# One block for three phases: the cross-attention's first loads, maxima and products moved in among the last steps of the self-attention

## The chip, the cores and the metric

The kernel runs on one core of a Trainium2 chip. The metric is the device time of one execution in microseconds, smaller being better. The core has TensorE (PE, matrix products, with its weight loads as PEld), VectorE (DVE), ScalarE (ACT), GpSimd (POOL) and SyncE (SP), which here only issues DMAs. Each engine works through its own list of instructions in order, and they meet at semaphores.

## The reference, cut to what matters

A decoder layer with normalisation after each part, over 32 sequences of 128 rows and 512 features:

```python
x = layernorm(x + attn(x, Wq, Wk, Wv, Wo))      # 16 heads of 32, rope, causal
x = layernorm(x + xattn(q=x, k=ctx, v=ctx))     # 8 heads; a head is 16 rows of the
                                                # sequence, and the 512 features take the
                                                # place of the positions
x = layernorm(x + ffn(x))                       # two ternary-weight layers, 512-2048-512
```

In `xattn` the scores of a head are a 512 by 512 matrix (contracted over 16 rows), so a sequence needs 8 such matrices, their row maxima, exponentials, and products with the values.

## The kernel before

The kernel has three phases: the self-attention, the cross-attention and the feed-forward. All loops are over the 32 sequences (`NB`) and are written out; inside a phase, `step(t)` of each engine works on several sequences at once, each at another stage.

The self-attention is a block of its own. Its results go to memory: `x1` (scratch x1), and `x1` and the context split in two parts of fewer bits (scratch x_part, c_part), in which the cross-attention later reads a head's rows as a stack. A block ends with all engines meeting: SP waits for the last stores (`x1_st`, `part_st`, `cpart_st`), and only then does the second block begin, which holds the cross-attention and the feed-forward. The order of work in the last steps of the self-attention is, on DVE: `out_low(31)` (L451), `norm_x1(30)` (L491), `residual(31)` (L475), `statistics(31)` (L479 to L484), `norm_x1(31)`. On PE: `attend(31)` (L599), `out_projection(31)` (L537). On POOL: `split_x1(30)` (L258, L293), `power(31)` (L300), `split_x1(31)`. On SP: x loads (L210), c_part stores (L214), x1 stores (L219) and x_part stores (L204). `norm_x1(b)` waits for the store of x1(b-1) to land, and `split_x1(b)` for the store of x_part(b-1), since each has one buffer.

The cross-attention's opening, in the second block, is:

- POOL fills the rows of ones: eight fills of 32 x 1024 in `cs` (L830) and two of 128 x 512 in `vT` (L834).
- SP loads four stacks, for sequences 0 and 1 in two groups of heads each: `load_stacks` issues eight DMAs for each (L739, L743), 768 KB by their shapes. Between them it loads ident, gamma and `cT`.
- For sequence 0, 16 units: PE forms two 512-wide products into a half of `wide` (`max_unit`, L987), and DVE takes their maxima (`pair_max`, L930). There are two halves, so PE is two units ahead at most.
- After unit 9, which needs the first nine maxima, PE transposes the first group's maxima (`transpose_max`, L994), ACT evicts them (L897), and POOL splits them (L857, L860) and writes them with four DMAs into the stacks (`store_max`, L867). Unit 10 waits for ACT's eviction.

Then the steady part begins: in a step of sequence b, eight `n` of four score tiles each (PE L1034, ACT's exponentials L906), products with the values (L1017), and the next sequence's 16 units of maxima between them. Its first scores wait for the first `store_max`, and those of n = 4 for the second one, `store_max(0, 0, 1)`, which POOL makes of maxima transposed after n = 0.

During steps 3 to 10 of the self-attention ACT also sums the magnitudes of the feed-forward's weights, into a tile `magnitude` of 2048 columns (L414).

Of the kernel before, what the change touches and what calls it, by code (L numbers as in the profile page):

```python
# [74 lines left out]
def self_attention(nc, NB, t_in, scratch, w_stage, w_abs):  # L75
# [5 lines left out]
    with ExitStack() as ctx:  # L81
        def sb(name, shape, dt=F32):
            return ctx.enter_context(nc.sbuf_tensor("a_" + name, shape, dt))

        def sem(name):
            return ctx.enter_context(nc.semaphore("a_" + name))

        stage = [w_stage[:, n * F:(n + 1) * F].rearrange("p (c n) -> p c n", c=KC) for n in range(4)]
        magnitude = sb("magnitude", [P, F])
        w_hi = sb("w_hi", [P, KC, 3 * D], F32R)  # L90
        w_lo = sb("w_lo", [P, KC, 3 * D], F32R)
        wo_hi = sb("wo_hi", [P, KC, D], F32R)
        wo_lo = sb("wo_lo", [P, KC, D], F32R)
        ident = sb("ident", [P, P])
        ident_b = sb("ident_b", [P, P], BF16)
        mask4 = sb("mask4", [P, HPC, P], BF16)
        cos = sb("cos", [P, DH])
        sin = sb("sin", [P, DH])
        xT = sb("xT", [P, D])
        xT_hi = sb("xT_hi", [P, KC, P], F32R)  # L100
        xT_lo = sb("xT_lo", [P, KC, P], F32R)
        x = sb("x", [P, D])
        q_raw = sb("q_raw", [P, D])
        q_sin = sb("q_sin", [P, D])
        q_rot = sb("q_rot", [P, D])
        k_sin = sb("k_sin", [P, D])
        k_cos = sb("k_cos", [P, D])
        k_rot = sb("k_rot", [P, D])
        v = sb("v", [P, KC, HPC, DH])
        qT = sb("qT", [P, KC, P])  # L110
        kT = sb("kT", [P, KC, P])
        neg_max = sb("neg_max", [P, HPC, KC])
        prob = sb("prob", [P, HPC, KC, P])
        probT = sb("probT", [P, HPC, KC, P])
        den = sb("den", [P, HPC, KC])
        rden = sb("rden", [P, HPC, KC])
        oT_hi = sb("oT_hi", [P, KC, P], F32R)
        oT_lo = sb("oT_lo", [P, KC, P], F32R)
        x1_sum = sb("x1_sum", [P, D])
        bn = sb("bn", [P, 6])  # L120
        mv = sb("mv", [P, 2])
        vare = sb("vare", [P, 1])
        neg_half = sb("neg_half", [P, 1])
        rstd = sb("rstd", [P, 1])
        x1 = sb("x1", [P, D])
        x1_part = sb("x1_part", [P, PARTS, D], F32R)
        c_in = sb("c_in", [P, D])
        c_part = sb("c_part", [P, PARTS, D], F32R)

        bank = [ctx.enter_context(nc.psum_tensor(f"a_bank{i}", [P, D], F32)) for i in range(8)]  # L130
        s_ps, (v_ps, q_ps, k_ps, o_ps) = bank[:4], bank[4:]

        w_ld = [sem(f"w_ld{n}") for n in range(4)]
        const_ld = sem("const_ld")
        w_hi_done = sem("w_hi_done")
        w_lo_done = sem("w_lo_done")
        pool_const = sem("pool_const")
        xT_ld = sem("xT_ld")
        x_ld = sem("x_ld")
        c_ld = sem("c_ld")  # L140
        x1_st = sem("x1_st")
        part_st = sem("part_st")
        cpart_st = sem("cpart_st")
        xT_hi_done = sem("xT_hi_done")
        xT_split = sem("xT_split")
        q_proj = sem("q_proj")
        k_proj = sem("k_proj")
        v_proj = sem("v_proj")
        q_raw_done = sem("q_raw_done")
        v_done = sem("v_done")  # L150
# [102 lines left out]
        def _(pool):  # L253
# [60 lines left out]
            def step(t, on):  # L314
# [4 lines left out]
                if on(0):  # L319
                    split_xT(t)  # L320
# [1642 lines left out]
```

## Time and profile before

| what | value |
|---|---|
| median of 3 runs | 1864.62 us (1862.95 to 1865.49) |
| the profiled execution's own time | 1859.43 us |
| its span, first to last instruction | 1857.6 us |
| PE busy | 1606.8 us (86%) |
| DVE busy | 1545.5 us (83%) |
| ACT busy | 1373.7 us (74%) |
| POOL busy | 959.0 us (52%) |
| mean granted TensorE clock | 0.931 |

The profile is of one execution, 0.3% shorter than the median run. Times in the trace count from the first instruction. A granted clock of 1.00 is 2.4 GHz, and 0.50 is 1.2 GHz; a value between is a stretch with both.

### The profile page before, as it was taken

The numbers are of one execution on the slowest core, as the hardware profiler recorded it, in microseconds if no ns is written. First come the engines' busy times: TensorE is split into PE (matmuls) and PEld (weight loads), VectorE is DVE, ScalarE is ACT, GpSimd is POOL, SyncE is SP. The second block draws the span as 40 slices with busy tenths as digits, with TensorE's granted clock in tenths as the row PEclk, the third lists the DMA queues.
The fourth block names the chain that finished last, engine by engine and source line by source line (L and its number), as shares of the span: only waits on it lengthen the run. The fifth ranks groups of instructions, "written<-read, shape, count | busy, mean of one in ns | idle before, by whom it ended". The sixth has DMA issues, their size and how long they took to land.

```text
span 1857.6 us, 35125 instructions
## 1 busy us (share of the span) xinstructions
PE 1606.8 (86%) x11936; PEld 873.5 (47%) x12000; DVE 1545.5 (83%) x2086; ACT 1373.7 (74%) x2837; POOL 959.0 (52%) x1407
## 2 busy tenths in 40 slices
PE   6999999999995498999999999999857777767784
PEld 4777777777774133333333333333323333333331
DVE  4778888888885597999999999999579999989985
ACT  4666654555553187888888888888789999989994
POOL 4666767767664443255553555423445555545552
PEclk9999999999998598999999999999988888888887
DMA  3455443443443445444456544444333333333311
GB/s 139 140 187 173 119 135 107 124 131 107 128 124 111 97 107 107 107 122 113 109 145 183 151 121 121 108 116 124 93 106 104 105 103 103 108 97 103 112 53 34
DMA packets 119268, 217.09 MB, mean 117 GB/s; under 512 B 32241, under 2 KB 34705, under 8 KB 116785
## 3 DMA queue, kind: packets, MB, share of 16 engines
q1 hardware_dynamic: 110770, 213.64, 40.8%
q0 software_dynamic: 8320, 1.21, 0.4%
q8 instruction: 96, 1.57, 0.4%
q14 instruction: 82, 0.67, 0.1%
HBM read 137.67 MB, written 76.02 MB: 115 GB/s over the span
## 4 chain that ended last, share of the span: by engine, by line
PE 32%; issue 11%; ACT 7%; DVE 6%; DMA 5%; POOL 4%; SPq 1%; POOLq 0%; DVEq 0%; ACTq 0%
PE sums L1017 13%; PE bank L1034 11%; PE wide L987 6%; DMA out<-c_result 3%; DVE stage L1658 2%; ACT stage L1543 2%; ACT b_prob L906 2%; DMA b_xs<-b_max_part 2%; DVE b_smax L930 1%; POOL c_up_rstd L1391 1%; DVE c_x L1645 1%; POOL c_mid_rstd L1426 1%; PE wide L994 1%; POOL b_xs L867 1%; DVE c_x_rnd L1699 1%
## 5 line engine op out<-in xcount | busy, mean ns | idle before, releaser
L930 DVE TENSOR_REDUCE b_smax<-wide 128x2 f32<-128x1024 f32 x512 | 620.3, 1225 | 67.5 <-PE wide L987 55.5
L906 ACT ACTIVATE b_prob<-bank 128x512 f32<-128x512 f32 x1024 | 556.3, 599 | 108.2 <-PE bank L1034 98.3
L1034 PE MATMUL bank<-b_xs,b_cs 50*128 50x512 f32 x1024 | 328.0, 475 | 22.5 <-ACT b_prob L906 12.8
L1017 PE MATMUL sums<-b_prob,b_vT 128*32 128x256 f32 (+1 forms) x3584 | 316.0, 424 | 5.5 <-ACT b_prob L906 0.5
L987 PE MATMUL wide<-b_cs,b_xs 48*128 48x512 f32 x1024 | 283.6, 439 | 37.7 <-DMA b_gamma<-in_gamma 30.9
L1836 PE MATMUL sums<-c_w,c_hqT 128*128 128x512 bf16 x481 | 168.9, 527 | 113.5 <-issue 104.0
L1034 PEld LDWEIGHTS bank<-b_xs,b_cs 50*128 50x128 f32 x1024 | 132.8, 186 | 230.2 <-ACT b_prob L906 168.6
L857 POOL TENSOR_SCALAR b_max_part<-b_neg_max 16x128 fp32r<-16x128 f32 x64 | 18.6, 290 | 337.0 <-ACT b_neg_max L897 337.0
L371 ACT ACTIVATE a_prob<-a_bank,a_neg_max 128x128 f32<-128x128 f32 x512 | 181.9, 418 | 3.6 <-DVE a_neg_max L459 3.6
L1836 PEld LDWEIGHTS sums<-c_w,c_hqT 128*128 128x128 bf16 x512 | 63.2, 128 | 209.1 <-issue 183.4
L987 PEld LDWEIGHTS wide<-b_cs,b_xs 48*128 48x128 f32 x1024 | 128.5, 191 | 64.8 <-POOL b_vT L834 31.3
L867 POOL DMA_DIRECT2D b_xs<-b_max_part x256 | 134.1, 530 | 42.1 <-POOL b_max_part L860 37.2
L1017 PEld LDWEIGHTS sums<-b_prob,b_vT 128*32 128x32 f32 x3584 | 72.6, 108 | 164.2 <-issue 106.6
L467 DVE TENSOR_TENSOR a_prob<-a_prob,a_rden 128x512 f32<-128x512 f32 x128 | 144.8, 1131 | 4.4
L349 ACT ACTIVATE a_v<-a_bank 128x512 f32<-128x512 f32 x32 | 19.1, 598 | 171.7 <-PE a_bank L599 171.7
L371 ACT ACTIVATION_READ_ACCUMULATOR a_prob<-a_bank,a_neg_max 128x1 f32 x512 | 132.3, 258 | 0.0
L1824 PE MATMUL wide<-c_w,c_xqT 128*128 128x512 bf16 x510 | 121.0, 392 | 0.5 <-issue 0.5
L537 PE MATMUL a_bank<-a_w_hi,a_xT_hi 128*128 128x512 f32 x384 | 108.2, 404 | 11.9 <-POOL a_xT_lo L269 11.9
L537 PE MATMUL a_bank<-a_w_lo,a_xT_hi 128*128 128x512 f32 x384 | 103.8, 392 | 0.0
L537 PE MATMUL a_bank<-a_w_hi,a_xT_lo 128*128 128x512 f32 x384 | 103.8, 392 | 0.0
L258 POOL TENSOR_SCALAR a_x_part<-a_x 128x512 fp32r<-128x512 f32 x32 | 19.9, 622 | 157.8 <-DMA scratch_x_part<-a_x_part 155.4
L587 PE MATMUL a_bank<-a_ident,a_prob 128*128 128x128 f32 x512 | 79.7, 282 | 10.1 <-DVE a_prob L467 9.4
(147 smaller groups left out, 3240.7 us busy)
## 6 DMA issues: line engine op xcount, KB each, us to landing
scratch_c_part<-a_c_part SPq DMA_DIRECT2D x64, 256.0 KB
scratch_x_part<-a_x_part SPq DMA_DIRECT2D x64, 256.0 KB
b_xs<-scratch_x_part SPq DMA_DIRECT2D x128, 128.0 KB, 3.1
b_cs<-scratch_c_part SPq DMA_DIRECT2D x128, 128.0 KB, 3.1
scratch_heads<-b_heads SPq DMA_DIRECT2D x64, 256.0 KB, 2.5
a_xT<-in_xT SPq DMA_DIRECT2D x32, 256.0 KB, 6.7
a_c_in<-in_ctx SPq DMA_DIRECT2D x32, 256.0 KB, 2.6
a_x<-in_x SPq DMA_DIRECT2D x32, 256.0 KB, 4.1
```

Source lines behind the costliest of these rows:

```text
L371: last = act.activation(prob[:, j, c, :], s_ps[j][:, c * P:(c + 1) * P], ACT.Exp, bias=neg_max[:, j, c:c + 1], accum_out=den[:, j, c:c + 1])
L467: dve.tensor_tensor(prob[:, j, :, :], prob[:, j, :, :], rden[:, j, :].unsqueeze(2).broadcast_to([P, KC, P]), ALU.mult).then_inc(norm_done, 1)
L537: last = pe.matmul(out, a[:, c, :], b[:, c, :], start=(n == 0), stop=(n == 3 * KC - 1))
L587: last = pe.transpose(s_ps[j][:, c * P:(c + 1) * P], prob[:, j, c, :], ident[:, :])
L867: pool.dma_start(xs[p][g][row:row + 1, :, :].rearrange("r h q -> r (h q)").bitcast(F32), max_part[g][2 * KC * e:2 * KC * (e + 1), j, :].bi ...
L906: act.activation(prob[k % 8][:, :], e_ps[bank_of(k)][:, :], ACT.Exp, scale=0.25).then_inc(exp_done, 1)
L930: dve.tensor_reduce(smax[g][:, :, j, qc], m_ps[u % 2][:, :, :], AX.X, ALU.max, negate=True).then_inc(max_done, 1)
L987: last = pe.matmul(m_ps[u % 2][:, e, :], xs[p][g][half(e, STACK), j, qc * P:(qc + 1) * P], cs[p][g][half(e, STACK), j, :], start=True, sto ...
L1017: last = pe.matmul(av_ps[2 * XD * h:2 * XD * (h + 1), cols], vT[p][:, lc, XG * g + h, :], prob[(XG * n + 2 * j + e) % 8][:, cols], start=( ...
L1034: pe.matmul(e_ps[bank_of(2 * u + e)][:, :], cs[p][g][half(e), j, lc * P:(lc + 1) * P], xs[p][g][half(e), j, :], start=True, stop=True).the ...
L1824: last = pe.matmul(h_ps[:, n, :], xqT[:, c, :], w1[:, c, n * D:(n + 1) * D], start=False, stop=(c == KC - 1))
L1836: last = pe.matmul(y_ps[:, :], hqT[:, c, :], w2[:, c, :], start=(c == 0), stop=(c == FC - 1))
```

## The change

The cross-attention's opening is handed to the self-attention as a function `begin` for each engine. The one block that is left has no meeting of the engines inside it. What moves, engine by engine:

- POOL: all ten fills stand ahead of everything else. `values(0, 0)` comes after step 33, `store_max(0, 0, 0)` after `power(31)`, and `split_x1(31)` behind that. Then POOL waits for all stores of the self-attention, writes four small constants and goes on with `store_max(0, 0, 1)`.
- SP: ahead of step 32 the stacks of sequence 0, ident, gamma and `cT`; ahead of step 33 one stack of sequence 1, and ahead of step 34 the other.
- PE: units 0 and 1 ahead of `out_projection(31)`, the 14 others behind it.
- DVE: maxima 0 to 3, `norm_x1(30)`, maxima 4 and 5, `residual(31)` and `statistics(31)`, maxima 6 to 9, `norm_x1(31)`, maxima 10 to 15.

What goes with it: `load_stacks` waits for the stores of its sequence, the feed-forward's loads wait for x1's, the score tiles of both attentions lie in the same PSUM tensor `wide`, the self-attention's tiles share their SBUF with tiles used later (`late`), and `magnitude` becomes a stack's tile of half the width, so that each sum of magnitudes is made in two halves.

```diff
     def sync(sp, begin):
...
             for t in range(NB, NB + 5):
+                begin(t - NB)
                 step(t, lambda k: t - k < NB)
-            sp.wait_ge(x1_st, 16 * NB)
-            sp.wait_ge(part_st, 16 * PARTS * NB)
-            sp.wait_ge(cpart_st, 16 * PARTS * NB)
...
     def gpsimd(pool, begin):
-            pipeline(pool, NB, 4, step)
+        for t in range(NB + 2):
+            step(t, lambda k: 0 <= t - k < NB)
+        begin(0)
+        step(NB + 2, lambda k: k > 2)
+        begin(1)
+        step(NB + 3, lambda k: k > 3)
...
     def scalar(act):
-                    act.activation(magnitude[:, :], w_stage[:, c * F:(c + 1) * F], ACT.Abs,
-                                   accum_out=w_abs[:, m, c:c + 1]).then_inc(ffn_summed, 1)
+                for half in range(2):
+                    at = c * F + half * F // 2
+                    if 2 * i + half > 0:
+                        act.wait_ge(ffn_summed, 2 * i + half)
+                    act.activation(magnitude, w_stage[:, at:at + F // 2], ACT.Abs,
+                                   accum_out=w_abs[:, m, 2 * c + half:2 * c + half + 1]).then_inc(ffn_summed, 1)
...
     def vector(dve, begin):
-            pipeline(dve, NB, 3, step)
+        for t in range(NB + 1):
+            step(t, lambda k: 0 <= t - k < NB)
+        out_low(NB - 1)
+        begin(0, 4)
+        norm_x1(NB - 2)
+        begin(4, 6)
+        residual(NB - 1)
+        statistics(NB - 1)
+        begin(6, 10)
+        norm_x1(NB - 1)
+        begin(10, XH * KC // 2)
...
     def tensor(pe, begin):
-            pipeline(pe, NB, 2, step)
+        for t in range(NB + 1):
+            step(t, lambda k: 0 <= t - k < NB)
+        begin(0, 2)
+        out_projection(NB - 1)
+        begin(2, XH * KC // 2)
...
def cross_attention(nc, ctx, NB, t_in, scratch, psum, sems, weights):
...
         def load_stacks(s, p, g):
+            sp.wait_ge(sems["part_st"], 16 * PARTS * (b + 1))
+            sp.wait_ge(sems["cpart_st"], 16 * PARTS * (b + 1))
+        def begin(k):
+            if k == 0:
                 sp.wait_ge(ones_done, 2)
                 load_stacks(0, 0, 0)
...
-        for g in range(2):
-            sp.wait_ge(ones_done, 6 + 2 * g)
-            load_stacks(0, 1, g)
+            if k in (1, 2):
+                sp.wait_ge(ones_done, 4 + 2 * k)
+                load_stacks(0, 1, k - 1)
...
     def gpsimd(pool):
+        def begin(k):
+            if k == 0:
                 values(0, 0, first=True)
+            if k == 1:
                 store_max(0, 0, 0, first=True)
+        def main():
+            for n in ("part_st", "cpart_st"):
+                pool.wait_ge(sems[n], 16 * PARTS * NB)
+            pool.wait_ge(sems["x1_st"], 16 * NB)
+            weights["of"].constants(pool)
...
     def tensor(pe):
+        def main():
+            pe.wait_ge(sems["sum_done"], NB)
             pairs(pe, pair)
```

## Rows read from the trace of the kernel before

**Rows 1.** The windows view: busy time, granted clock (PEclk), DMA share, GB/s

```profile
613.00:640.65 27.65, 12.15 (x33) 4.92 (x35) 16.75 (x16) 0.27 (x1) 12.53 (x21) 0.50 0.72 137
```

**Rows 2.** The waits, 560 to 640 us: total, times, longest

```profile
PE wide L987 <- DMA b_gamma<-in_gamma: 30.9, 1, 30.9
POOL a_x_part L258 <- DMA scratch_x_part<-a_x_part: 21.8, 3, 9.4
```

**Rows 3.** The timeline, all engines, 585 to 640 us: start, duration, engine, line

```profile
587.73 0.69 DVE L451 TENSOR_TENSOR a_oT_lo<-a_bank,a_oT_hi 128x512 fp32r<-128x512 f32 x1 [0.67 <-ACT a_oT_hi L386]
587.95 3.08 SPq L204 DMA_DIRECT2D scratch_x_part<-a_x_part  x2
...
590.49 1.08 PE L537 MATMUL a_bank<-a_wo_hi,a_oT_lo 128*128 128x512 f32 x4
594.09 0.55 DVE L491 TENSOR_SCALAR a_x<-a_x_sum,a_mv,a_rstd 128x512 f32<-128x512 f32 x1 [5.66 <-DMA scratch_x<-a_x]
...
594.77 0.69 DVE L475 TENSOR_TENSOR a_x_sum<-a_bank,a_x 128x512 f32<-128x512 f32 x1
...
596.55 0.15 DVE L484 TENSOR_SCALAR a_vare<-a_mv 128x1 f32<-128x1 f32 x1
597.08 0.62 POOL L258 TENSOR_SCALAR a_x_part<-a_x 128x512 fp32r<-128x512 f32 x1 [9.38 <-DMA scratch_x_part<-a_x_part]
...
599.00 0.56 POOL L300 TENSOR_TENSOR a_rstd<-a_vare,a_neg_half 128x1 f32<-128x1 f32 x1
...
605.34 0.62 POOL L258 TENSOR_SCALAR a_x_part<-a_x 128x512 fp32r<-128x512 f32 x1 [5.78 <-DMA scratch_x_part<-a_x_part]
...
613.03 7.96 POOL L830 MEMSET b_cs<- 32x1024 f32 x8 [5.72 <-POOLq L81]
...
615.00 0.80 SPq L739 DMA_DIRECT2D b_xs<-scratch_x_part  x2
...
621.05 1.12 POOL L834 MEMSET b_vT<- 128x512 f32 x2
...
622.50 1.22 PE L987 MATMUL wide<-b_cs,b_xs 48*128 48x512 f32 x4 [30.92 <-DMA b_gamma<-in_gamma]
...
623.40 11.41 DVE L930 TENSOR_REDUCE b_smax<-wide 128x2 f32<-128x1024 f32 x10 [10.21 <-PE wide L987]
...
634.60 0.29 POOL L857 TENSOR_SCALAR b_max_part<-b_neg_max 16x128 fp32r<-16x128 f32 x1 [6.29 <-ACT b_neg_max L897]
...
635.39 9.15 DVE L930 TENSOR_REDUCE b_smax<-wide 128x2 f32<-128x1024 f32 x8 [0.58 <-PE wide L987]
636.08 2.35 POOL L867 DMA_DIRECT2D b_xs<-b_max_part  x4 [0.66 <-POOL b_max_part L860]
```

**Rows 4.** SP's waits, 500 to 640 us

```profile
SPq L198 <- POOL a_c_part L293: 39.8, 4, 11.4
```

**Rows 5.** The windows view: n = 0 to 3 of sequence 0, then 4 to 7

```profile
640.65:653.19 12.54, 12.54 (x75) 4.65 (x71) 10.38 (x10) 8.56 (x17) 5.36 (x8) 0.68 0.01 1
653.19:663.90 10.71, 10.39 (x93) 3.94 (x89) 10.00 (x9) 9.56 (x19) 6.71 (x7) 1.00 0.35 101
```

**Rows 6.** The timeline again: the second group's maxima, scores of n = 4

```profile
644.53 0.29 POOL L857 TENSOR_SCALAR b_max_part<-b_neg_max 16x128 fp32r<-16x128 f32 x1 [6.10 <-ACT b_neg_max L897]
...
653.23 0.50 PE L1034 MATMUL bank<-b_xs,b_cs 50*128 50x512 f32 x2
```

**Rows 7.** The timeline of the kernel's first microseconds

```profile
7.64 2.29 DVE L431 TENSOR_TENSOR a_w_lo<-stage,a_w_hi 128x2048 fp32r<-128x2048 f32 x1 [7.64 <-ACT a_w_hi L335]
...
9.37 1.05 POOL L258 TENSOR_SCALAR a_xT_hi<-a_xT 128x512 fp32r<-128x512 f32 x1 [8.55 <-DMA a_mask<-in_mask]
```

**Rows 8.** The page's groups: busy, mean ns, idle before and its releaser

```profile
L349 ACT ACTIVATE a_v<-a_bank 128x512 f32<-128x512 f32 x32 | 19.1, 598 | 171.7 <-PE a_bank L599 171.7
```

**Rows 9.** All instructions of line 414

```profile
L414 ACT ACTIVATE a_magnitude<-stage x8: 1911/1936/1947, 75.2 to 197.4; 128x2048 f32<-128x2048 f32 x8
```

**Rows 10.** The waits, 690 to 760 us

```profile
PE bank L1034 <- DMA b_xs<-b_max_part: 4.5, 1, 4.5
```

More of the change, by code:

```diff
@@ L701, in cross_attention, with late @@
     MAX_LOADS = 2 * PARTS
+    prob, heads = [], []
+    def late():
+        prob.extend(sb(f"prob{i}", [P, D]) for i in range(8))
+        heads.extend(sb(f"heads{g}", [P, D]) for g in range(2))
     def after(s, p):
@@ L788, in step @@
                 load_stacks(s + 1, p, 0)
-            weights.load(sp, s, p, 0)
+            weights["of"].load(sp, s, p, 0)
             if not first:
@@ L821, in rest, with ones @@
                 store_rden(NB - 1)
-        return rest
-    def gpsimd(pool):
+        return begin, main, rest
+    def ones(pool):
         n = 0
@@ L836, in gpsimd @@
             pool.wait_ge(ones_done, n)
-        weights.constants(pool)
+    def gpsimd(pool):
         def values(s, p, first=False):
@@ L970, in rest @@
                 reciprocals(NB - 1)
-        return rest
+        return begin, main, rest
     def tensor(pe):
@@ L1063, in pair, with begin, main @@
             step(s, 1, False, first, last)
-        pe.wait_ge(ones_done, 10)
-        pe.wait_ge(const_ld, 32)
-        for u in range(PAIRS):
-            max_unit(0, 0, u, first=True, after_mt=1 if u == 10 else None)
-            if u == 9:
-                transpose_max(0, 0, 0, 9)
-        pairs(pe, pair)
-        for part in range(2):
-            products(NB // 2 - 1, 1, STEPS - 1, part)
-    return sync, gpsimd, scalar, vector, tensor
+        def begin(u, to):
+            if u == 0:
+                pe.wait_ge(ones_done, 10)
+                pe.wait_ge(const_ld, 32)
+            while u < to:
+                max_unit(0, 0, u, first=True, after_mt=1 if u == 10 else None)
+                if u == 9:
+                    transpose_max(0, 0, 0, 9)
+                u += 1
+        def main():
+            pe.wait_ge(sems["sum_done"], NB)
+            pairs(pe, pair)
+            for part in range(2):
+                products(NB // 2 - 1, 1, STEPS - 1, part)
+        return begin, main
+    return late, ones, (sync, gpsimd, scalar, vector, tensor), xs[1][1]
 def feed_forward(nc, ctx, NB, t_in, scratch, stage, w_abs, psum, sems, out):
@@ L1295, in prepare @@
             if slot == 4:
-                self.fold(pool, w_abs, KC, 0)
+                self.fold(pool, w_abs, 2 * KC, 0)
                 for m in range(2):
@@ L1885, in _ @@
         def _(sp):
-            ffn[0](sp, attn[0](sp))
+            begin, main, rest = attn[0](sp)
+            own[0](sp, begin)
+            main()
+            ffn[0](sp, rest)
         @block.gpsimd
         def _(pool):
-            attn[1](pool)
+            ones(pool)
+            begin, main = attn[1](pool)
+            own[1](pool, begin)
+            main()
             ffn[1](pool)
@@ L1894, in _ @@
         def _(act):
+            own[2](act)
             attn[2](act)
@@ L1899, in _ @@
         def _(dve):
-            ffn[3](dve, attn[3](dve))
+            begin, main, rest = attn[3](dve)
+            own[3](dve, begin)
+            main()
+            ffn[3](dve, rest)
         @block.tensor
         def _(pe):
-            attn[4](pe)
+            begin, main = attn[4](pe)
+            own[4](pe, begin)
+            main()
             ffn[4](pe)
```

1027 lines of the change are left out of this document (515 added, 512 removed).

## The prediction

> **What bounds the kernel now.** I began with the windows view. In each attention's steady part PE sets the pace: n = 0 to 7 of the first sequence of the cross-attention take 12.54 and 10.71 us with PE busy for 12.54 and 10.39 of them [rows 5]. Between the phases it does not: from the second block's start at 613.0 to the first scores at 640.65 PE is busy for 12.15 of 27.65 us, at the lower clock [rows 1]. The waits name the largest hole: PE stood still for 30.9 us before the first maxima's products [rows 2].
>
> The timeline shows what fills that hole. PE's last self-attention product starts at 590.49 and takes 1.08. Behind it runs a chain that uses almost no engine: x1(29)'s store lands at 594.09, DVE normalises and adds until 596.70, POOL splits x1(30) at 597.08 when x_part(29)'s store has landed, its next split waits until 605.34 for x_part(30), and the block ends when x_part(31) has landed; the fills start at 613.03 [rows 2, 3]. Then come ten fills (9.1 us with those of `vT`), the loads, and at 622.50 the first unit. From 623.40 DVE sets the pace: ten maxima in 11.41 us, 1.14 each [rows 3].
>
> **What the change removes.** I follow DVE, since the opening's 16 maxima must all pass through it, and compare the start of maximum 10, which is at 635.39 now [rows 3]. After the change:
>
> - `out_low(31)` ends at 588.42. Units 0 and 1 are by then on PE, which is free behind `attend`, and their stacks were loaded long before. Maxima 0 and 1: until 590.71.
> - Unit 2 stands behind `out_projection(31)`, which ends at 591.57. From unit to maximum it takes 0.90 (622.50 to 623.40), so maxima 2 and 3 run from 592.47 to 594.76 [rows 3].
> - `norm_x1(30)` can run, x1(29) having landed at 594.09. With 0.6 for it: 595.36. Maxima 4 and 5: 597.65.
> - `residual(31)` and `statistics(31)` took 594.77 to 596.70, or 1.93, so 599.6. Maxima 6 to 9: 604.2. `norm_x1(31)`: 604.8.
> - Maximum 10 waits for PE's transpose and ACT's eviction. That path now takes 1.72 from maximum 8's end (623.40 + 9 x 1.141 = 633.67) to 635.39; here from 603.05 to 604.77. It is covered by maximum 9 and the norm [rows 3].
>
> So maximum 10 starts at 604.8, which is 30.6 us earlier, and PE's first scores follow at 610.05 in place of 640.65. Everything behind them keeps its order and moves along. This is the large term: **-30.6**.
>
> **What it adds.** Three chains must be ready for that, and SP and POOL are now shared.
>
> SP: ahead of step 32 it issues 19 DMAs, at 0.46 each 8.7 us (0.80 for the two of [rows 3], and a gap). It waited there up to 11.4 us for the context's split [rows 4], which I take as the cover; without it step 32's loads would be 8.7 us late. Ahead of steps 33 and 34 stand eight DMAs each, 3.7 us. The first eight lie in the wait for `sum_done` behind step 32. The second eight push x_part(29)'s two stores from 587.95 to 591.6. They landed 9.1 us after 587.95 [rows 3]; I keep that figure, so they land at 600.8. It is a choice between 6.3 (x_part(30) was issued as POOL's split ended at about 599.0 and had landed by 605.34), which gives 597.9, and 9.1 plus the stall of the second store's issue again (3.08 for two issues, in place of 0.9), which gives 602.9.
>
> POOL: `split_x1(30)` then takes 600.8 to 602.7 (597.08 to 599.00 before), `power(31)` until 603.3. `norm_x1(31)` wants it at 604.2 and `store_max(0, 0, 0)` wants POOL at 634.60 - 30.6 = 604.0, so 0.7 us is to spare. If x_part(29) lands at 597.9, more; if at 602.9, the opening loses 1.4. I take **0**.
>
> POOL again: x_part(30) is issued at 602.7 and lands 6.3 later, at 609.0; its split ends at 611.0, and x_part(31) lands 5.7 to 6.3 later (before, at most 613.03 - 607.30). POOL stands in front of `store_max(0, 0, 1)` until 616.7 to 617.3, add 0.2 for the constants. From POOL's copy to the first use it took at most 640.65 - 634.60 = 6.05 [rows 3], so its rows are ready at 622.95 to 623.55. The scores of n = 4 came 12.58 after the first ones [rows 5, 6], so they want them at 622.63. Before, this `store_max` began at 644.53, 8.7 us ahead of its use [rows 6]. The new wait on stores costs 0.3 to 0.9; I take the low side, since 6.05 is an upper bound: **+0.3**. Behind POOL's wait stand `values(0, 1)`, needed only a whole step later (12.54 + 10.71 us [rows 5]), and the weights' preparation.
>
> The kernel's start: ten fills of 9.1 us from 0.72 end at 9.8; the first split of xT starts at 9.37 now, beside DVE's subtraction (7.64 to 9.93), and takes 1.05, where the same copy of x1 takes 0.62 [rows 3, 7]. At 9.9 it no longer runs beside it: +0.2 at the least. If DVE's subtraction slows the fills as it slows that copy (1.05 / 0.62, over its 2.3 us), they end 0.9 later: +1.1. PE's first product hangs on that split, with nothing to hide it. I take the middle, **+0.6**.
>
> The shared port has a rule in the Trainium skill (SBUF — State Buffer, Who interferes with whom): a DVE instruction with two SBUF inputs contends with a GpSimd instruction that reads SBUF, not with one that only writes. The trace's 1.05 for the copy beside the subtraction agrees; the fills only write, so by the rule the term would be +0.2 and the sum -30.1.
>
> Magnitudes in halves: eight passes of 1.94 us [rows 9] become sixteen of at least half that, with one more fixed start and a wait each. If each half cost as much as a whole, ACT would have 1.9 us more in eight steps. It idles 171.7 / 32 = 5.4 us a step before `values`, right behind these passes [rows 8]: **0**. Without that idle time it would be 15 us. The two waits in each `load_stacks` are on counts long reached, and one more fold of `w_abs` falls into POOL's idle time (POOL is at 13 of 27 us even in the opening [rows 1]): 0.
>
> The sum is -30.6 + 0.3 + 0.6 = **-29.7 us**. Against the profiled execution's span of 1857.6 this is 1827.9, and its own time is 1.8 longer. The median of the runs shown lies 5.2 above the profiled time (0.3%), so I set the difference against the median: 1864.62 - 29.7 = **1834.9 us**.
>
> **The rivals.**
>
> *POOL's and DVE's chain becomes late.* A store that lands after 601.5 in place of 600.8 costs a microsecond per microsecond, at `power(31)`, and again at the second `store_max`, two stores further. For it: x_part(29) took 9.1, and 768 KB of loads now run ahead of it. Against: the DMA share had room. With 602.9 for the first and 8 in place of 6.3 for the next two, the sum loses 5 to 6: 1840.5. Chance 0.22.
>
> *The first scores' own DMA lands late.* The small stores of maxima are in flight together with x_part(30). Later in the kernel PE waits 4.5 us for one of them [rows 10]; the same here gives 1839.4. Chance 0.06. The Trainium skill (DMA: Bandwidth & Descriptors, Queues, rings and completion order) says that a completion lands only after every earlier write of that DMA engine, across its queues. The 4.5 us fit, but no row here tells that cause from another.
>
> *The clock stays up.* PE now works through the hole, and the main part may begin at the upper clock. The first four n took 12.54 us at a mean clock of 0.68 (half speed for 8.0 us), the next four 10.71 [rows 5]: a gain of 1.8, or 3 if counted with the product that n = 0 lacks. Against: busy for 12.15 of 27.65 us PE stayed at 0.50 [rows 1], and the new order gives it the same two products per maximum. It gives 1832.5. Chance 0.12.
>
> *The loads crowd out the self-attention's own transfers.* Window 613 to 640.65 moved 137 GB/s at a share of 0.72 [rows 1], so four stacks (3.1 MB) fill the DMA engines for 16 us. Laid wholly onto the last steps this returns 16 us, half of it 8: about 1847 in the middle. Against: they are spread over 35 us. Chance 0.08.
>
> *Nothing overlaps:* DVE stands at `norm_x1(30)` with the maxima behind it, until the stores have gone as late as now. The opening then ends where it did: 1864. Chance 0.02.
>
> *Slower: the clock stays down.* If PE, never rested but never full, stays at half speed after the first scores, each microsecond so spent costs 1.83 / 8.0 = 0.23, or 3 / 8.0 = 0.37. It decides from 80 to 130 us of half speed beyond the 8 of now; 170 us of it give 1874 to 1898. Against: PE at full duty came back to 1.00 within the first four n [rows 5]. Chance 0.03.
>
> **How the numbers follow.** The forecast as worked out has 0.47; the rivals 0.22, 0.06, 0.12, 0.08, 0.02 and 0.03. Low end: the clock's 3 us, the start at +0.2, no wait at the stores, and 2 to 3 us of difference between executions (the three runs span 2.5): 1828. High end: 1840.5 with the start at +1.1 and the executions' spread: 1843. That leaves out crowding, no overlap and the slow case, and a little of each side. A difference under 0.2% can't be told from none. Faster: 0.95; within 0.2%: 0.02; slower: 0.03.
>
> **What would show it.** Right: the maxima L930 start near 588.5 and number 10 near 605; the first scores 30 us earlier; `xT_hi` at about 9.9; `store_max(0, 0, 1)` near 617, just in time. PE has no hole of over 5 us near 600. Wrong: DVE idle before `norm_x1(30)` or `(31)` for a DMA, POOL's second `store_max` after 620 with PE waiting at n = 4, last self-attention steps longer than before, or another granted clock in the later phases, which the sum takes as unchanged and which alone could move the time by several microseconds.

## The result, and the profile after

The changed kernel took 1834.56 us (median of 4 runs, 1833.18 to 1843.81) against 1865.05 for the one before (4 runs, 1862.95 to 1869.94) on the same chip: a ratio of 0.985, 95% interval 0.983 to 0.987. The profiled execution took 1833.27 us with a span of 1831.5. A second comparison with more runs (`r1_change`: 6 against 23) gives 1833.02 against 1862.14, ratio 0.985 (0.982 to 0.989). The forecast was 1834.9, faster.

The timeline of the changed kernel for DVE, 585 to 625 us. It answers to [rows 3]; line 969 is the maximum (930 before), 493 the norm of x1, 477 the residual.

```profile
585.03 0.69 DVE L477 TENSOR_TENSOR a_x_sum<-sums,a_x 128x512 f32<-128x512 f32 x1 [1.87 <-PE sums L549]
...
588.25 2.35 DVE L969 TENSOR_REDUCE b_smax<-wide 128x2 f32<-128x1024 f32 x2
591.94 2.36 DVE L969 TENSOR_REDUCE b_smax<-wide 128x2 f32<-128x1024 f32 x2 [1.35 <-PE wide L1029]
594.24 0.55 DVE L493 TENSOR_SCALAR a_x<-a_x_sum,a_mv,a_rstd 128x512 f32<-128x512 f32 x1
594.71 2.35 DVE L969 TENSOR_REDUCE b_smax<-wide 128x2 f32<-128x1024 f32 x2
...
598.81 4.61 DVE L969 TENSOR_REDUCE b_smax<-wide 128x2 f32<-128x1024 f32 x4
...
604.00 6.88 DVE L969 TENSOR_REDUCE b_smax<-wide 128x2 f32<-128x1024 f32 x6
```

The gap of 5.66 us before `norm_x1(30)` is gone: the maxima fill it, and DVE is busy for 22.30 of the 24.91 us from 585 to the first scores. Maximum 10 starts at 604.00, where [rows 3] have 635.39.

The same timeline for POOL and SP: the split of x1 is line 253, `store_max` 885 to 895, the stores of x_part 201, the stacks' loads 764 and 768.

```profile
588.19 2.65 SPq L764 DMA_DIRECT2D b_xs<-scratch_x_part  x2
590.89 1.60 SPq L768 DMA_DIRECT2D b_cs<-scratch_c_part  x2
...
594.39 1.20 SPq L201 DMA_DIRECT2D scratch_x_part<-a_x_part  x2
...
600.69 0.62 POOL L253 TENSOR_SCALAR a_x_part<-a_x 128x512 fp32r<-128x512 f32 x1 [12.43 <-DMA scratch_x_part<-a_x_part]
...
602.62 0.56 POOL L295 TENSOR_TENSOR a_rstd<-a_vare,a_neg_half 128x1 f32<-128x1 f32 x1
603.22 0.29 POOL L885 TENSOR_SCALAR b_max_part<-b_neg_max 16x128 fp32r<-16x128 f32 x1
...
608.56 0.61 POOL L253 TENSOR_SCALAR a_x_part<-a_x 128x512 fp32r<-128x512 f32 x1 [1.37 <-issue]
...
616.82 0.29 POOL L885 TENSOR_SCALAR b_max_part<-b_neg_max 16x128 fp32r<-16x128 f32 x1
```

The stores' chain has not become shorter; the wait that was at the block's end is now spent inside the cross-attention, and POOL comes to the second `store_max` at 616.82. PE's side, same timeline: the first scores and those of n = 4 (line 1076).

```profile
609.91 0.80 PE L1076 MATMUL bank<-b_xs,b_cs 50*128 50x512 f32 x2 [0.44 <-DMA b_xs<-b_max_part]
...
621.70 0.50 PE L1076 MATMUL bank<-b_xs,b_cs 50*128 50x512 f32 x2
```

Its waits, 560 to 640 us, answer to [rows 2]. PE's wait of 30.9 us is gone; what is left is DVE's pace.

```profile
POOL a_x_part L253 <- DMA scratch_x_part<-a_x_part: 23.5, 3, 12.4
...
PE wide L1029 <- DVE b_smax L969: 7.6, 10, 2.3
...
POOL c_neg_half L1324 <- DMA scratch_x_part<-a_x_part: 6.1, 1, 6.1
```

The windows view (PE, PEld, DVE, ACT, POOL busy, granted clock, DMA share, GB/s): first the clock around 596 and after 616 us, then the first four n and the next four, as in [rows 5].

```profile
594.00:596.00 2.00, 0.52 (x4) 0.21 (x4) 2.00 (x4) 0.00 (x0) 0.00 (x0) 0.99 0.84 178
596.00:598.00 2.00, 1.57 (x4) 0.56 (x4) 1.97 (x3) 0.00 (x0) 0.00 (x0) 0.50 0.68 189
...
616.00:618.00 2.00, 2.00 (x22) 0.51 (x14) 1.08 (x2) 0.75 (x2) 0.89 (x6) 0.89 0.13 48
...
609.91:621.70 11.79, 11.41 (x73) 5.05 (x74) 9.91 (x10) 8.43 (x17) 4.93 (x13) 0.72 0.26 70
621.70:632.40 10.70, 10.37 (x93) 3.91 (x89) 10.00 (x9) 9.55 (x19) 7.93 (x8) 1.00 0.37 101
```

The clock still falls to 0.50 in the opening, at about 596 us (594 before), and returns in the first four n.

### The profile page after: what moved, and what is told of

Read it like the earlier page. It is cut to its first block, busy times and chain, and to the rows that moved or that the text cites. A ratio compares the mean times of both kernels' runs of the same rounds, so it can differ in the third digit from the quotient of the medians.

```text
span 1831.5 us, 35203 instructions
## 1 busy us (share of the span) xinstructions
PE 1609.7 (88%) x11936; PEld 873.5 (48%) x12000; DVE 1546.8 (84%) x2086; ACT 1377.0 (75%) x2853; POOL 961.4 (52%) x1408
## 4 chain that ended last, share of the span: by engine, by line
PE 58%; issue 12%; DVE 10%; ACT 7%; DMA 6%; POOL 5%; SPq 1%; POOLq 0%; DVEq 0%; ACTq 0%
PE sums L1059 13%; PE bank L1076 12%; PE bank L549 11%; PE wide L1029 6%; PE sums L549 5%; DMA out<-c_result 3%; PE wide L599 3%; DVE stage L1710 2%; ACT stage L1595 2%; PE wide L591 2%; ACT b_prob L945 2%; DVE a_prob L469 2%; PE sums L611 2%; DMA b_xs<-b_max_part 2%; PE wide L586 1%
## 5 line engine op out<-in xcount | busy, mean ns | idle before, releaser
L370 ACT ACTIVATE a_prob<-wide,a_neg_max 128x128 f32<-128x128 f32 x512 | 181.8, 417 | 3.9 <-DVE a_neg_max L461 3.9
L348 ACT ACTIVATE a_v<-bank 128x512 f32<-128x512 f32 x32 | 19.1, 598 | 168.9 <-PE sums L611 168.9
L370 ACT ACTIVATION_READ_ACCUMULATOR a_prob<-wide,a_neg_max 128x1 f32 x512 | 132.3, 258 | 0.0
L549 PE MATMUL bank<-a_w_hi,a_xT_hi 128*128 128x512 f32 x384 | 107.8, 403 | 12.4 <-POOL a_xT_lo L264 12.4
L549 PE MATMUL bank<-a_w_lo,a_xT_hi 128*128 128x512 f32 x384 | 103.7, 392 | 0.0
L549 PE MATMUL bank<-a_w_hi,a_xT_lo 128*128 128x512 f32 x384 | 103.0, 390 | 0.0
L599 PE MATMUL wide<-a_ident,a_prob 128*128 128x128 f32 x512 | 80.8, 283 | 10.8 <-DVE a_prob L469 10.0
```

The source lines that it names most:

```text
L370: last = act.activation(prob[:, j, c, :], s_ps[j][:, c * P:(c + 1) * P], ACT.Exp, bias=neg_max[:, j, c:c + 1], accum_out=den[:, j, c:c + 1])
L549: last = pe.matmul(out, a[:, c, :], b[:, c, :], start=(n == 0), stop=(n == 3 * KC - 1))
L599: last = pe.transpose(s_ps[j][:, c * P:(c + 1) * P], prob[:, j, c, :], ident[:, :])
```

## The experiments

An execution of this kernel scatters by several us ahead of the change (the runs `e8_parts_first` and `e9_before_parts_first` say where from), so the traces are compared over one stretch that holds the change and little of that scatter: from DVE's start of `residual(30)` to the first product of scores. Before it is 585.13 to 640.65, 55.52 us; after, 585.03 to 609.91, 24.88; in `r1_change`, 588.40 to 613.52, 25.12.

**The change again** (`r1_change`, no edit), to have the size with more runs.

> The changed kernel itself, so that its relation to the kernel before and its spread are known on this chip. The trace showed the first scores at 609.9 us in place of 640.65 (30.7 earlier), but a span only 26.1 shorter, while the medians differ by 30.5. If the 4.6 us lost behind the first scores belong to the change, this run's profile shows them again and the ratio stays near 0.984; if they are the difference of one execution from another, the first scores come again near 610 and the span is 1827 to 1835.

It gave 1833.02 against 1862.14 us, as above. Its first scores came at 613.52 us, later than in the change's first profile, since the self-attention's steps were longer; from them to the last instruction it took 1216.9 us, as long as in the kernel before (1217.0), where the change's first profile took 1221.6. The 4.6 us that were missing in that profile are thus a difference between executions, not the change's.

**The maxima last** (`e2_maxima_last`). DVE keeps the self-attention's last steps whole and takes all 16 maxima behind them; fills and loads stay early. (POOL's `begin(1)` moves behind its last step with them; PE's order stays.)

```diff
         step(NB + 2, lambda k: k > 2)
+        step(NB + 3, lambda k: k > 3)
         begin(1)
-        step(NB + 3, lambda k: k > 3)
...
         out_low(NB - 1)
-        begin(0, 4)
         norm_x1(NB - 2)
-        begin(4, 6)
         residual(NB - 1)
         statistics(NB - 1)
-        begin(6, 10)
         norm_x1(NB - 1)
-        begin(10, XH * KC // 2)
+        begin(0, XH * KC // 2)
```

> Everything as in the change, but DVE does out_low, both norms, residual and statistics first and all 16 maxima behind norm_x1(31). Theory (the opening is a chain of 16 maxima on DVE, laid into its waits for stores): maxima begin at about 603.9, when power(31) has passed, number 10 at 615.9, the first scores at about 621.2 in place of 609.9, so 11.3 us slower than the change: 1846 us, 0.990 of the kernel before. Rival (early fills and loads and the missing meeting of the engines give the whole gain, the interleaving nothing): the time of the change, 1835 us.

It took 1847.49 us, ratio to before 0.993 (0.990 to 0.997). The stretch is 588.02 to 623.44, 35.42 us, 10.5 more than with the change (11.3 were expected). DVE's timeline shows the idle time come back:

```profile
596.96 0.55 DVE L493 TENSOR_SCALAR a_x<-a_x_sum,a_mv,a_rstd 128x512 f32<-128x512 f32 x1 [5.64 <-DMA scratch_x<-a_x]
...
605.73 0.55 DVE L493 TENSOR_SCALAR a_x<-a_x_sum,a_mv,a_rstd 128x512 f32<-128x512 f32 x1 [6.15 <-POOL a_rstd L295]
606.19 11.40 DVE L966 TENSOR_REDUCE b_smax<-wide 128x2 f32<-128x1024 f32 x10
```

So 10.5 us of the gain are maxima laid into DVE's waits for a store and for POOL.

**Everything last** (`e3_all_last`). One block still, but fills, first loads and maxima all behind the self-attention, so that only the meeting between the two blocks is gone. (DVE and PE take all maxima and units last, and POOL's fills, `ones`, stand in its `begin(-1)`.)

```diff
         for t in range(NB, NB + 5):
-            begin(t - NB)
             step(t, lambda k: t - k < NB)
+        for k in range(3):
+            begin(k)
...
-        begin(0)
         step(NB + 2, lambda k: k > 2)
-        begin(1)
         step(NB + 3, lambda k: k > 3)
+        pool.wait_ge(x1_split, 2 * NB)
+        begin(-1)
+        begin(0)
+        begin(1)
...
```

> One block, but fills, loads, products and maxima all behind the self-attention's own work, in the old order; only the meeting of the engines is gone. Theory: the fills start when POOL's last split has ended, near 607.4 in place of 613.0, the first scores come at about 635.0, and the kernel takes 1859.5 us (0.997 of the kernel before). Then the 30.7 us divide into 5.6 for the meeting, 13.8 for early fills and loads, 11.3 for the interleaved maxima. Rival (the meeting is the cost, since it holds all engines for the last stores): 15 us or more are gained by this alone, under 1850.

It took 1862.45 us, ratio 1.000 (0.997 to 1.003). Its stretch is 601.22 to 652.90, 51.68 us: 3.8 less than before, and 16.3 more than with the maxima last. The timeline shows POOL's fills and SP's first load at once behind the last split, which ended at 623.19, where [rows 3] have the fills at 613.03, 5.72 us after POOL's last work:

```profile
623.25 7.97 POOL L857 MEMSET b_cs<- 32x1024 f32 x8
...
625.23 1.30 SPq L763 DMA_DIRECT2D b_xs<-scratch_x_part  x2
...
634.80 1.22 PE L1030 MATMUL wide<-b_cs,b_xs 48*128 48x512 f32 x4 [27.14 <-DMA b_gamma<-in_gamma]
```

From the fills to the first unit it now takes 11.55 us, against 622.50 - 613.03 = 9.47 before, which gives back 2.1 of the 5.7. The loads here run beside x_part(31)'s store; that this is the reason is argued, not shown. The three traces share out the 30.6 us: the meeting 3.8, fills and loads ahead of time 16.3, maxima between the norms 10.5. The shares that were expected were 5.6, 13.8 and 11.3. The whole kernel's time does not show the 3.8: that would be a ratio of 0.998, which lies within the interval, and in this profile most steps of the self-attention took 18.20 us. So the 3.8 rest on one profile's stretch. The rival, that the meeting alone costs 15 us or more, is ruled out by the time as well.

**The stack's loads later** (`e5_stores_later`): both lots of loads of the next sequence ahead of step 34, thus all in front of x_part(29)'s store.

```diff
         for t in range(NB, NB + 5):
-            begin(t - NB)
+            if t != NB + 1:
+                begin(t - NB)
+            if t == NB + 2:
+                begin(1)
             step(t, lambda k: t - k < NB)
```

> As the change, but both stacks of sequence 1 are loaded ahead of step 34, so that x_part(29) is stored 3.7 us later still. Theory (POOL's chain of stores had under 1 us to spare): split_x1(30) near 604.4 in place of 600.7, norm_x1(31) waits for power(31) until 607, the first scores at about 613.3, and the second store of maxima costs 1 us more: 3.4 to 4.6 us slower than the change, 1838 to 1840. Rival (the store chain has several us to spare, and the sum was right by chance): no difference to the change, within 1 us.

It took 1841.58 us, ratio 0.988 (0.985 to 0.992), an interval that overlaps the change's. The stretch is 583.08 to 612.41, 29.33 us, 4.4 more. The timeline:

```profile
603.17 0.62 POOL L256 TENSOR_SCALAR a_x_part<-a_x 128x512 fp32r<-128x512 f32 x1 [16.93 <-DMA scratch_x_part<-a_x_part]
...
607.43 0.80 PE L1032 MATMUL wide<-b_cs,b_xs 48*128 48x512 f32 x2 [5.01 <-DVE b_smax L972]
...
612.41 0.80 PE L1079 MATMUL bank<-b_xs,b_cs 50*128 50x512 f32 x2 [0.79 <-DMA b_xs<-b_max_part]
...
619.37 0.29 POOL L888 TENSOR_SCALAR b_max_part<-b_neg_max 16x128 fp32r<-16x128 f32 x1
```

This is the first rival's mechanism, brought about by an edit: a split that is late holds `power(31)`, `norm_x1(31)` and the maxima behind it. It is also a bound for the second `store_max`: begun 6.96 us after the first scores (619.37 - 612.41), as against 6.91 with the change, it too made no wait at n = 4.

**The stores first** (`e4_stores_first`, one execution): x_part(29)'s store in front of the second lot of loads.

```diff
-            begin(t - NB)
+            if t < NB + 2:
+                begin(t - NB)
             step(t, lambda k: t - k < NB)
+            if t == NB + 2:
+                begin(2)
```

> The change, but the second stack of sequence 1 is loaded behind step 34 and not ahead of it, so that x_part(29) is stored 3.7 us earlier. Theory (the store chain is on time, with about 0.7 us to spare): split_x1(30) at about 597 in place of 600.7, but the first scores come as late behind residual(30) as in the change (24.9 us) within 0.5 us, as DVE's chain sets them. Rival (the chain was on the critical path): they come 2 to 4 us earlier.

One run took 1830.16 us, which tells nothing by itself. The stretch is 586.46 to 610.66, 24.20 us, 0.7 to 0.9 less. The timeline:

```profile
589.64 3.03 SPq L201 DMA_DIRECT2D scratch_x_part<-a_x_part  x2
...
598.49 0.62 POOL L256 TENSOR_SCALAR a_x_part<-a_x 128x512 fp32r<-128x512 f32 x1 [8.86 <-DMA scratch_x_part<-a_x_part]
...
604.61 0.29 POOL L888 TENSOR_SCALAR b_max_part<-b_neg_max 16x128 fp32r<-16x128 f32 x1 [3.65 <-ACT b_neg_max L939]
...
610.66 0.63 PE L1079 MATMUL bank<-b_xs,b_cs 50*128 50x512 f32 x2
```

POOL now waits 3.65 us for ACT before `store_max`, so the split has that much to spare, where the change has next to none. But maximum 10 comes no sooner after `residual(30)` (605.39 - 586.46 = 18.93, against 604.00 - 585.03 = 18.97). What is gained lies behind it: the scores do not wait for the maxima's own small DMA, for which they waited 0.44 us in the change's profile and 0.69 in `r1_change`. That is from one profile, and too small to be seen in the time.

**PE kept busy** (`e6_pe_kept_busy`): two products more behind each unit from the second on, whose results nobody reads.

```diff
                 max_unit(0, 0, u, first=True, after_mt=1 if u == 10 else None)
+                if u >= 1:
+                    for e in range(2):
+                        pe.matmul(e_ps[e][:, :], xs[0][0][half(e, STACK), 0, 0:P], cs[0][0][half(e, STACK), 0, :],
+                                  start=True, stop=True)
```

> The change, with two more products of 512 columns behind each unit of the opening from unit 1 on, into two PSUM banks that nobody reads and that the first scores write anew. Theory (the first scores run at half clock, since PE has rested): if PE's clock stays at 1.00 through the opening, n = 0 to 3 take 10.7 us in place of 11.8, and the kernel gains 1 to 2 us. Rival (at half speed the added products make PE the slower of the two, 1.66 us a unit against DVE's 1.14): if the clock falls in any case, the opening is up to 7 us longer.

It took 1836.9 us, ratio 0.986 (0.983 to 0.990), with a stretch of 25.52 us: no gain, and not the 7 us longer opening of the rival either. In the timeline the units of two products take 0.50 us until PE rests for 2.33 us, from 606.1, and 0.80 after it:

```profile
608.44 0.80 PE L1029 MATMUL wide<-b_cs,b_xs 48*128 48x512 f32 x2 [2.33 <-DVE b_smax L969]
```

**The weights' sums early** (`e7_sums_early`). After the change one more hole stands in the cross-attention: PE waits 4.3 us for a small DMA of the maxima, and the clock falls with it ([rows 10] have 4.5). Just before, POOL stores two columns of 4 bytes a partition. This run moves that fold and its stores into the self-attention.

```diff
             step(t, lambda k: 0 <= t - k < NB)
+            if t == 2 * KC + 6:
+                pool.wait_ge(ffn_summed, 4 * KC)
+                begin("sums")
...
-            if slot == 4:
-                self.fold(pool, w_abs, 2 * KC, 0)
-                for m in range(2):
-                    pool.dma_start(scratch["w_sums"][m].rearrange("(p one) -> p one", one=1), w_abs[:, m, 0:1]).then_inc(
-                        w_sum_st, 16)
...
```

> The change, with the fold of the weights' sums and their two stores to memory (4 bytes for each of 128 partitions) moved from the third sequence of the cross-attention into the self-attention, where POOL issues no DMA that anyone waits for. Theory: in the third sequence these stores hold the DMA engines for some 8 us, a store of maxima lands late, PE waits 4.5 us and then runs 8 us at half clock; without them the sequences of maxima 48 to 80 take 2 x 21.3 us in place of 26 and 25, and the kernel gains 8 us: 1826 us. Rival (the broadcast load of the sums, which stays where it is, or the stacks' loads are the cause): the 4.5 us remain, and the time is that of the change.

The changed kernel's timeline and windows around the hole, 663 to 685 us:

```profile
663.07 1.20 POOL L1349 DMA_DIRECT2D scratch_w_sums<-w_abs  x2 [0.29 <-POOL w_abs L1336]
...
672.76 1.15 POOL L1354 DMA_DIRECT2D c_w_total<-scratch_w_sums  x2 [1.53 <-DMA scratch_w_sums<-w_abs]
...
679.17 0.80 PE L1076 MATMUL bank<-b_xs,b_cs 50*128 50x512 f32 x2 [4.32 <-DMA b_xs<-b_max_part]
```

```profile
680.00:685.00 5.00, 5.00 (x29) 1.91 (x28) 2.45 (x2) 2.79 (x6) 0.49 (x2) 0.50 0.29 61
```

With the sums early that wait is not there at all (655 to 760 us), and the stretch of maxima 32 to 80 is 7.2 us shorter against the change. Yet the time was 1835.74 us, ratio 0.985 (0.982 to 0.988), the change's own. In the profiled execution the first scores came at 616.69 us, 6.8 later than in the change's profile: several self-attention steps were long, and one took 21.19 us. The next runs show that this was not the sums' doing alone.

**The stores of x_part first in each step** (`e8_parts_first`, and `e9_before_parts_first`, the same edit in the kernel before). The self-attention's steps take 17.25 to 18.1 us in both kernels, though PE has about 17.25 us of work in each (it is busy for 17.30 of the 17.59 us of the step shown below). POOL's 27 waits for x_part's landing (below) suggested a ring: POOL splits x1, takes q's rotation and the context's split, SP waits for that split to load the next context, and only behind that load stores x_part, for which POOL's next split waits.

```diff
-            if on(1):
-                b = t - 1
-                if later(b):
-                    sp.wait_ge(c_split, 2 * b)
-                sp.dma_start(c_in[:, :], rows(t_in["ctx"], b)).then_inc(c_ld, 16)
             if on(5):
...
                         part_st, 16)
+            if on(1):
+                b = t - 1
+                if later(b):
+                    sp.wait_ge(c_split, 2 * b)
+                sp.dma_start(c_in[:, :], rows(t_in["ctx"], b)).then_inc(c_ld, 16)
```

> The change, with one edit to the self-attention's SP order: x_part is stored ahead of the context's load instead of behind it. Why: one kernel's profiles show self-attention steps of 17.25 to 18.2 us. In the changed kernel POOL's split of x1 waits for x_part's store, whose issue waits on SP for the context's split, which stands behind the split of x1 on POOL: 2.0 + 1.0 + 4.9 + 2.7 us on POOL, and 0.4 + 6.3 for issue and landing, a ring of about 17.3 us beside PE's 17.25. Theory (that ring makes the steps longer and the times scatter): the steps fall to 17.25 to 17.3, the first scores come 8 to 9 us earlier, the kernel takes about 1825 us and its runs scatter less than the 5 us of now. Rival (PE alone sets the step, and the scatter is the clock's): no difference to the change.

> The same edit in the kernel before, which has the same ring. Theory: its steps fall from a mean of 17.5 to 17.3 us and it takes 1853 to 1856 us (0.995 to 0.997), so the difference that the change makes, measured without the ring, is again 30 us: 1855 to 1825. Rival: no difference, and the scatter of the kernel before stays.

The edit in the changed kernel gives 1822.25 us (1817.73 to 1838.2), ratio 0.979 (0.976 to 0.982); in the kernel before, 1854.35 (1847.39 to 1862.34), ratio 0.995 (0.993 to 0.997). POOL's waits from 60 to 560 us, the longest in sum, of the changed kernel:

```profile
POOL a_x_part L253 <- DMA scratch_x_part<-a_x_part: 136.6, 27, 5.5
```

and of `e8_parts_first`:

```profile
POOL a_q_sin L276 <- ACT a_q_raw L341: 129.7, 29, 4.5
```

The starts of two neighbouring residuals on DVE, of the changed kernel (17.59 us apart):

```profile
411.49 0.69 DVE L477 TENSOR_TENSOR a_x_sum<-sums,a_x 128x512 f32<-128x512 f32 x1 [1.19 <-PE sums L549]
429.08 0.69 DVE L477 TENSOR_TENSOR a_x_sum<-sums,a_x 128x512 f32<-128x512 f32 x1 [1.19 <-PE sums L549]
```

and of `e8_parts_first` (17.26):

```profile
405.44 0.69 DVE L477 TENSOR_TENSOR a_x_sum<-sums,a_x 128x512 f32<-128x512 f32 x1 [1.18 <-PE sums L549]
422.70 0.69 DVE L477 TENSOR_TENSOR a_x_sum<-sums,a_x 128x512 f32<-128x512 f32 x1 [1.19 <-PE sums L549]
```

POOL's wait has moved to its input from PE and ACT, and the steps are PE's: it is busy for 17.22 of the 17.26 us. By the medians that is worth 9 us in the kernel before and 11 to 12 in the changed one, and it has nothing to do with the change: between the two kernels with the edit the difference is 32.1 us (1854.35 to 1822.25).

One part of the expectation failed. The runs were to scatter less, and they do not: six executions of `e8_parts_first` span 20.5 us and nine of `e9_before_parts_first` 15.0, against 10.7 for the 14 of the kernel before beside them (and 18.4 for the 23 beside `r1_change`). The rival had named the clock, and for what is left the record fits it: the execution of 1838.2 us had a mean granted clock of 0.923, the one of 1817.73 us 0.934. The first is the profiled one, with every steady step at 17.23 to 17.27 us, and it lost its time later. The windows from the last maximum to the end, of the changed kernel and of `e8_parts_first`:

```profile
1286.70:1831.50 544.80, 391.56 (x1952) 183.71 (x1985) 451.22 (x741) 477.18 (x452) 263.04 (x586) 0.82 0.30 93
```

```profile
1284.96:1836.30 551.34, 408.24 (x1985) 184.63 (x1985) 452.09 (x740) 477.43 (x452) 261.08 (x586) 0.80 0.30 92
```

It takes 6.5 us more there at the lower clock, and 5.5 more between the first scores and the last maximum. Why the clock differs from one execution to the next is not shown.

**Both** (`e10_parts_sums`), **and with PE kept busy in the opening's holes** (`e11_parts_sums_busy`: two products behind each unit, twelve behind unit 7, four behind unit 15).

```diff
...
                 max_unit(0, 0, u, first=True, after_mt=1 if u == 10 else None)
+                if u >= 1:
+                    for n in range({7: 6, 15: 2}.get(u, 1)):
+                        for e in range(2):
+                            pe.matmul(e_ps[e][:, :], xs[0][0][half(e, STACK), 0, 0:P], cs[0][0][half(e, STACK), 0, :],
+                                      start=True, stop=True)
```

> The change with both edits: x_part stored ahead of the context's load (alone 1822 us, 0.979) and the weights' sums stored from within the self-attention (alone 1835.7 us, though its profile regains 7.2 us in the third sequence of the cross-attention and loses 3.6 us in one self-attention step of 21.2 us, where the small stores delay x_part's). Theory: with the ring of POOL and x_part's store opened, a late store costs the self-attention nothing, so the two gains add: 1822 - 7 = 1815 us, 0.975. Rival: the small stores hold up all DMAs wherever they stand, and the step of 21 us comes again: 1819 us or more.

> As the run with both edits, and PE kept busy through the opening: two added products behind each unit, twelve behind unit 7, where PE otherwise rests 2.3 us and lost its clock in the earlier try, and four behind unit 15. Theory: the clock stays at 1.00 up to the first scores, n = 0 to 3 take 10.7 in place of 11.8 us, and 1 to 2 us are gained: 1813.5 us. Rival: it falls all the same, or the added products delay the units: no gain, 1815 us or more.

`e10_parts_sums` took 1816.41 us (1809.38 to 1828.31), ratio 0.977 (0.974 to 0.980), and its profile has neither a long self-attention step (the 29 steady ones are 17.07 to 17.27) nor PE's wait at the third sequence. Its interval overlaps that of `e8_parts_first`, so what the early sums add is seen in the profiles, 7.2 us, and not settled by the times. `e11_parts_sums_busy` took 1816.37 us, ratio 0.975 (0.972 to 0.978): no difference that can be told from none. Its windows show that the clock fell all the same, at 586.2 us. Two products had by then been added behind each unit from the second on; the twelve start only at 589.4.

```profile
585.00:586.00 1.00, 0.66 (x4) 0.23 (x4) 1.00 (x2) 0.00 (x0) 0.00 (x0) 1.00 0.51 107
586.00:587.00 1.00, 0.94 (x4) 0.40 (x4) 1.00 (x3) 0.00 (x0) 0.00 (x0) 0.60 0.84 238
587.00:588.00 1.00, 0.53 (x4) 0.35 (x4) 1.00 (x2) 0.00 (x0) 0.00 (x0) 0.50 0.68 127
...
610.00:612.00 2.00, 2.00 (x24) 0.78 (x24) 1.85 (x2) 1.66 (x4) 1.73 (x4) 0.97 0.07 12
```

What a steady upper clock in the opening is worth thus stays open; no run reached it.

## Why the prediction was right, step by step

The mechanism came as forecast, and its large term was measured. That 1834.9 and 1834.56 lie 0.3 us apart is luck beyond that: the two comparisons give differences of 30.5 and 29.1 us, single executions of the change range over 20 us, and one of the first four, 1843.81, lay above the forecast's high end.

**What is removed (-30.6).** Each step of the walk along DVE came within 0.8 us. Maxima 0 and 1 start at 588.25 (588.42 forecast), 2 and 3 at 591.94 (592.47), `norm_x1(30)` at 594.24 (594.76), maxima 6 to 9 at 598.81 (599.6), maximum 10 at 604.00 (604.8), the first scores at 609.91 (610.05). The trace's difference is 30.7 us. In the first scores an error hides another: maximum 10 was 0.8 us early, but from it to them it took 5.91 us where I carried over 640.65 - 635.39 = 5.26; 0.44 of the 0.65 are the wait for the small DMA. The second rival's mechanism is thus there, at about a tenth of its price, and the profile of `e4_stores_first` is without it.

**SP.** The first lot of 19 DMAs took from 556.77 to 567.76, 11.0 us and not 8.7, and the context's load followed at 568.07: the cover of 11.4 us in [rows 4] held, with almost nothing left of it. The second lot of eight was mis-sized as well: I had it end at 591.6, and it ended at 594.35, its first two issues taking 2.65 us and the next two 1.60. But x_part(29) then landed 6.3 us after its issue, not 9.1, and the two errors cancel: 600.69 against 600.8. The rows of both bounds were read rightly, but the upper one counted a stall twice, since the 9.1 us of [rows 3] run from the start of an issue that itself took 3.08. `e4_stores_first` shows the pair again: issued in front, the store has the 3.03 us and the 8.85 us. From the issue's end the landing took 6.05, 5.82 and, in the change, 5.10 us, so most of the difference is the long issue. That it strikes whoever comes first at this place is my reading of these three traces; what fills up there no run shows.

**POOL.** `power(31)` at 602.62 and `store_max(0, 0, 0)` at 603.22 were to be 602.7 and 604.0; the chain had almost nothing to spare, as forecast, and `e5_stores_later`, whose split is at 603.17, shows the first rival's price when it has not: 4.4 us. The second `store_max` began at 616.82 (616.7 to 617.3 forecast). The term of +0.3 was mis-sized: it measured 0. PE has no wait at n = 4, and `e5_stores_later`, where this `store_max` began 6.96 us after the first scores, has none either. The first four n took 11.79 us and not 12.54, so the use came at 621.70, and even so the rows were there.

**The clock.** The forecast kept it as before, and in the main it is: 0.50 from about 596 to 616.4. It came back 6.5 us after the first scores instead of 8.0, and by my estimate from the two levels that is the 0.7 us by which the first four n were shorter. It does not belong to the change: in `r1_change`, the same kernel, it came back after 8.1 us. Nor does it follow how busy PE was in the opening: after 6.9 us in `e2_maxima_last`, with PE busy for 10.94 of the 24.9 us before the first scores, and after 8.2 in `e11_parts_sums_busy`, with 21.71. The rival "the clock stays up" did not occur, and two attempts to bring it about failed.

**The start (+0.6).** PE's first product came at 12.39 us, 0.53 later than before, and at 12.38 to 12.40 in all nine other runs with early fills; in `e3_all_last`, whose fills are late, it came at 11.69. The middle was right for the wrong reason. The timeline of the start:

```profile
7.58 2.29 DVE L433 TENSOR_TENSOR a_w_lo<-stage,a_w_hi 128x2048 fp32r<-128x2048 f32 x1 [7.58 <-ACT a_w_hi L334]
8.75 1.12 POOL L862 MEMSET b_vT<- 128x512 f32 x2
...
10.33 0.61 POOL L253 TENSOR_SCALAR a_xT_hi<-a_xT 128x512 fp32r<-128x512 f32 x1 [0.31 <-POOL a_neg_half L249]
```

The fills beside DVE's subtraction were no slower than in [rows 3] (1.12 us for those of `vT`), as the rule of the Trainium skill (SBUF — State Buffer, Who interferes with whom) has it for a GpSimd instruction that only writes, and the split takes 0.61 instead of 1.05. The fills ended at 9.87; behind them a small memset and a gap take until 10.33, which I had not counted. By the time of the first rotated k the difference can't be seen: 22.11 us before, 21.46 to 22.48 in the changed kernel and its variants. So the term was there at the first product, and what it cost the whole kernel is not shown.

**The others.** Loads did not crowd the last steps out: `residual(30)` stands at 585.03 against 585.13, and from 60 to 585 us PE is busy for 511.17 us against 512.40. The profiled span gained less than the opening, 26.1 against 30.7 us: 1.5 of the rest are lost by the last maximum, and 3 in the feed-forward part, where the granted clock was 0.82 against 0.83 before. The medians do not have that loss (30.5), and neither has the profile of `r1_change`.

## What to carry to other kernels

Where two phases meet, follow the engine through which the opening's work must pass, and ask which of its idle times are waits for a store's landing: work of the next phase laid there cost nothing here, and that and the early fills and loads were 27 of the 30.6 us. Where an issue takes long, ask whether the landing's time already contains it, and don't count both. And look in the steady part for a wait, step after step, on the landing of the engine's own last store: a one-line change of order was worth a third of this change. Last, a forecast that comes within a microsecond of a kernel whose executions spread over 20 has its steps confirmed by the trace, not by the time.

## What the runs showed that was not expected

- Ahead of the opening, scatter came from a ring of waits of about PE's own length. In the nine profiles with the old order (`e3_all_last` included) `residual(30)` began between 583.1 and 601.2 us; in the four with x_part's store issued ahead of the wait it began between 574.2 and 577.4, with steady steps of 17.07 to 17.27 us. Behind the first scores another scatter stays, 1208 to 1234 us from there to the end over all profiles; of the two profiles of the changed kernel the longer one (1221.6 against 1216.9 us) has the lower granted clock. The forecast's spread of 2 to 3 us was too small: `r1_change` ranged from 1827.3 to 1848.03.
- Two stores of 4 bytes a partition were issued at 663.07 us; their read-back could only start at 672.76. The next maxima's small DMA made PE wait 4.32 us until 679.17; without them that part was 7.2 us shorter, the clock's fall included. Issued at 254 us, in the self-attention, they lengthened no step in the profile of `e10_parts_sums`. The Trainium skill (DMA: Bandwidth & Descriptors, Queues, rings and completion order) says that a completion lands only after all earlier writes of the same DMA engine; the wait agrees, but the runs show only that the stores' absence removes the wait, not through which of the DMA's parts they caused it.
- The clock fell in the opening at about 596 us after 2 us with PE busy for 0.52 of them, in `e6_pe_kept_busy` at 606.1, just as PE's rest of 2.33 us began, and in `e11_parts_sums_busy` at 586.2, with PE busy for 0.66 of the us before and 0.94 of the us in which it fell. Products added between dependent units did not hold it.
